# Expert tiles inside the late attention batches of a fused attention and mixture-of-experts kernel

## The chip, the core and the metric

One NeuronCore of a Trainium2 chip runs the whole program. The metric is the device time in microseconds (us) of one execution. PE is TensorE, DVE is VectorE, ACT is ScalarE, POOL is GpSimd, SP is SyncE.

## What is computed

The input x has 8 batches of 256 positions with 256 features in fp32. The output is x plus an attention branch plus a mixture-of-experts branch, both fed with the layer-normalised x:

```
xn  = layernorm(x)
qkv = xn @ Wqkv.T + b              # 16 query heads of 16; one key head and one value head of 16
A   = softmax(causal(q k^T / 4)) v @ out_w.T + out_b
p   = softmax(xn @ w_router.T);  top 4 of 16 experts, weights normalised to sum 1
M   = sum over chosen e of coeff_e * (silu(xn @ w_gate[e]) * (xn @ w_up[e])) @ w_down[e]
out = x + A + M
```

There are 2048 tokens and four choices for each. The choices are sorted by expert into tiles of 128 rows, of which there are MT = 79 at most.

## The kernel before

The program is written by hand, engine by engine, with counted semaphores. An engine runs its list strictly in order. It has three stages.

Front (0 to about 88 us). `normalise`, `project` and the router work in four groups of 512 tokens. Keys go to DRAM as `k_d`, queries as `q_d`, normalised rows as `xn_d`. SP loads keys back in two transfers of four pieces (`load_k`, L330), and POOL copies them out, five and four times, into `ks` (`copy_k`, L472). `load_q` (L335) loads a batch's queries in eight issues of 128 KB. DVE's routing (`choose`, `sum_over_tiles`, `slot_numbers`) ends the front.

Attention (about 88 to 217 us). `batch(b)` runs over 8 batches of NB = 12 slots. In each slot s, PE does one score block for the row maxima of a batch that is 18 slots ahead (`scores_for_max`, L638; DVE takes its maximum, L1194) and one score block of this batch (`scores`, L653; ACT takes Exp, L925). The first kind alternates between PSUM banks 0 and 1, the second between banks 3 and 4. Between them stand, at fixed slots: `weigh_v` (L664, s = 1, 5, 9), `context` (L676, s = 3, 8), `transpose_context` (L686, s = 1, 9), `project_out` (L692, s = 3, 11), `transpose_max` (L644, s = 7), and on ACT and DVE the copies that these need (`keep_context` L931, `keep_cxt` L936, `normalise_context`, `add_out`, `split_max`). `load_m` (L373) returns the maxima, and `load_q(b + 3)` follows when the scores of batch b are done. In slots 14 to 29 `list_rows` (L700) makes the lists of rows; POOL's one-hot tables for it (L499) have HOTS = 14 places in the room of the weights of experts 6 to 11. ACT issues the weights of two experts in each batch (`load_experts`, L951), three transfers of 512 KB.

Tile loop (221 to 486 us). For tile j: POOL gathers 128 rows (`gather`, L512); PE transposes them (`tile_xT`, L775), ACT copies them (L990); PE multiplies by gate and up weights of the tile's expert (`tile_gate_up`, L785); ACT takes Silu (`tile_silu`, L986); DVE multiplies by up and coefficient (`tile_h`, L1285); PE transposes (`tile_hT`, L793), DVE copies (L1292); PE multiplies by the down weights (`tile_down`, L801), two tiles behind; ACT copies (`tile_y`, L997); POOL adds the rows into `out` (even j) or `odd_d` (odd j) with an accumulating indirect transfer (`send`, L526). `gather(j)` waits until `tile_h` of tile j - 4 is done, and POOL's order is gather(j + 3), send(j - 2). `send(0)` waits until SP has stored x plus attention of all batches (L399). After the last send one accumulating transfer adds `odd_d` to `out` (L545).

Of the kernel before, what the change touches and what calls it, by code (L numbers as in the profile page):

```python
# [33 lines left out]
def attention_and_experts(nc, x, wqkv, bqkv, wout, bout, wrouter, wgate, wup, wdown, out):  # L34
# [22 lines left out]
    HOTS = 14  # L57
# [9 lines left out]
    q_d = nc.dram_tensor("q_d", (2 * B, 2, KC, P, HALF), F32).ap()  # L67
# [3 lines left out]
    with ExitStack() as ctx:  # L71
# [9 lines left out]
        with nc.sbuf_tensor("wgu_low", [P, (E - 4) * KC, 2 * F], F32) as wgu_low:  # L81
            with nc.sbuf_tensor("qs_wgu", [P, 2, H, HALF], F32R) as qs_wgu:
                pass
        wgu = sb("wgu", [P, E * KC, 2 * F])
        wdn = sb("wdn", [P, E * FC, D])
        HOT_E = 6
        hot = wgu[:, HOT_E * KC:(HOT_E + 6) * KC, :].rearrange("p r f -> p (r f)").bitcast(F16)
        hot_p = hot[:, 0:HOTS * TOP_K * P].rearrange("p (r k c) -> p r k c", r=HOTS, k=TOP_K)
        hot_j = hot[:, HOTS * TOP_K * P:HOTS * TOP_K * (P + MTE)].rearrange("p (r k c) -> p r k c", r=HOTS, k=TOP_K)
# [22 lines left out]
        after_q = sb("after_q", [P, NU, P])  # L112
        wqT = sb("wqT", [P, KC, D])
        wvrkT = sb("wvrkT", [P, KC, 48])
# [5 lines left out]
        stats = sb("stats", [P, NT, 6])  # L120
        mv = sb("mv", [P, NT, 2])
        var_e = sb("var_e", [P, NT])
        std0 = sb("std0", [P, NT])
        rstd = sb("rstd", [P, NT])
        logits = sb("logits", [P, NT, E])
        probs = sb("probs", [P, NT, E])
        rowstat = sb("rowstat", [P, NT])
        top_w = sb("top_w", [P, NT, 8])
        top_e = sb("top_e", [P, NT, 8], U32)
        top_ef = sb("top_ef", [P, NT, TOP_K])  # L130
        iota_e = sb("iota_e", [P, E])
        onehot = out_buf[:].rearrange("p (t k e) -> p t k e", t=NT, k=TOP_K)
        chosen = sb("chosen", [P, NT, E], BF16)
        PADT = NT // 2
        scan_t = sb("scan_t", [P, 2, PADT + NT, E])
        PADE = E // 2
        scan_e = sb("scan_e", [P, 2, PADE + E])
        ntile_i = sb("ntile_i", [P, E], I32)
        first_row = sb("first_row", [P, E])
        slot_i = sb("slot_i", [P, NT, TOP_K], I32)  # L140
        slot_p = sb("slot_p", [P, NT, TOP_K], I32)
        slot_f = sb("slot_f", [P, NT, TOP_K])
# [4 lines left out]
        tile_no = sb("tile_no", [1, MT])  # L147
        tile_ge = scan_t[0:1].rearrange("p a t e -> p (a t e)").bitcast(BF16)[:, 0:MT * E].rearrange("p (j e) -> p j e", j=MT)
        tile_ef = sb("tile_ef", [1, MT])
        tile_e = sb("tile_e", [1, MT], I32)  # L150
        slots = sb("slots", [P, MT], I32)
        get_row = sb("get_row", [P, MT], I32)

# [145 lines left out]
        def _(sp):  # L299
# [51 lines left out]
            for g in range(NG):  # L351
# [15 lines left out]
                if g == 1:  # L367
                    load_k(0, GW)
# [968 lines left out]
```

## Time and profile before

| | |
|---|---|
| time, median of 3 runs | 504.11 us (503.55 to 506.36) |
| the profiled execution's own time | 504.1 us |
| its span in the trace | 502.4 us |
| PE busy | 418.8 us, 83% |
| POOL busy | 294.8 us, 59% |
| DVE busy | 226.0 us, 45% |
| ACT busy | 179.8 us, 36% |
| transfers | 57.17 MB, mean 114 GB/s |

Busy times are sums over stages with different limits, so they don't say what bounds a stage. The chain of work that ended last does: it is followed back from the last instruction, at each step to what released it. Its shares are PE 36%, issue 19%, POOL 16%, DVE 12%, DMA 8%. "Issue" is time in which an engine waited for nothing that the profile shows.

### The profile page before, as it was taken

What the parts mean: (1) busy time and instruction counts of PE and PEld (TensorE: products, weight loads), DVE (VectorE), ACT (ScalarE), POOL (GpSimd) and SP (SyncE); (2) the same over time, 40 slices, a digit from 0 to 9 for tenths busy, and PEclk for the clock granted to TensorE, in tenths of its full rate; (3) what the DMA queues carried; (4) which work ended last, traced back from release to release, by engine and by line L of the source; (5) the groups of instructions that cost most, each with busy time, mean ns of one, the idle gap of its engine ahead of it and who ended that gap; (6) DMA issues with size and microseconds to landing.
All of it is one profiled execution on the core that took longest, in us unless ns stands there. A gap on an engine that the chain in (4) does not pass through costs nothing.

```text
span 502.4 us, 6742 instructions
## 1 busy us (share of the span) xinstructions
PE 418.8 (83%) x1672; PEld 227.8 (45%) x1673; DVE 226.0 (45%) x555; ACT 179.8 (36%) x424; POOL 294.8 (59%) x298
## 2 busy tenths in 40 slices
PE   4896083888889888879899999999999999999920
PEld 2242031434544544435565555555555555555510
DVE  5987688468767666413232222222222222222210
ACT  2353100337745556633333333333333333333310
POOL 7953130998511100303888888888888888888740
PEclk9889555559999999999999999999999999999985
DMA  7668796344876792642544444454544455446217
GB/s 218 228 180 189 179 131 97 126 80 136 167 151 165 179 187 86 213 147 64 78 76 81 82 79 77 77 82 76 84 74 75 84 85 82 75 77 81 38 22 146
DMA packets 54034, 57.17 MB, mean 114 GB/s; under 512 B 11376, under 2 KB 48928, under 8 KB 53760
## 3 DMA queue, kind: packets, MB, share of 16 engines
q0 software_dynamic: 15440, 21.51, 25.6%
q1 hardware_dynamic: 25904, 22.87, 20.9%
q10 hardware_dynamic: 12672, 12.58, 8.4%
q8 instruction: 7, 0.11, 0.1%
q14 instruction: 11, 0.09, 0.1%
HBM read 37.40 MB, written 23.33 MB: 121 GB/s over the span
## 4 chain that ended last, share of the span: by engine, by line
PE 36%; issue 19%; POOL 16%; DVE 12%; DMA 8%; SPq 4%; ACT 3%; ACTq 0%; POOLq 0%
POOL late L512 10%; PE bank L785 9%; PE bank L801 5%; PE bank L664 4%; PE bank L638 4%; PE bank L653 4%; POOL odd_d L526 3%; PE bank L692 3%; DVE pmax L1194 3%; POOL out_dram L526 3%; DMA late<-xn_d,get_row 2%; PE bank L676 2%; DVE early L1051 2%; PE bank L775 2%; DMA q_d<-early 2%
## 5 line engine op out<-in xcount | busy, mean ns | idle before, releaser
L785 PE MATMUL bank<-wgu,late 128*128 x316 | 152.2, 604 | 3.0 <-issue 1.2
L512 POOL DMA_INDIRECT late<-xn_d,get_row x79 | 83.2, 1053 | 69.2 <-PE bank L653 27.6
L1285 DVE SCALAR_TENSOR_TENSOR late<-late,bank 128x256 f32<-128x256 f32 x79 | 37.9, 480 | 154.5 <-ACT late L986 154.5
L925 ACT ACTIVATE pt<-bank 128x512 f32<-128x512 f32 x96 | 56.0, 599 | 79.3 <-PE bank L653 78.3
L801 PE MATMUL bank<-wdn,late 128*128 x316 | 81.5, 381 | 1.4 <-DVE late L1292 1.4
L1194 DVE TRANSPOSE_TENSOR_REDUCE pmax<-bank 128x16 f32<-128x512 f32 x96 | 66.5, 706 | 33.7 <-PE bank L638 32.7
L986 ACT ACTIVATE late<-bank 128x256 f32<-128x256 f32 x79 | 30.3, 383 | 130.8 <-PE bank L785 130.8
L785 PEld LDWEIGHTS bank<-wgu,late 128*128 128x128 f32 x316 | 53.7, 189 | 46.7 <-issue 45.5
L526 POOL DMA_INDIRECT out_dram<-late,slots x40 | 63.5, 1588 | 19.1 <-issue 10.4
L526 POOL DMA_INDIRECT odd_d<-late,slots x39 | 61.9, 1587 | 12.8 <-issue 9.8
L801 PEld LDWEIGHTS bank<-wdn,late 128*128 128x128 f32 x316 | 53.9, 190 | 6.4 <-issue 2.4
L499 POOL TENSOR_SCALAR wgu<-iota_p,slot_pf 128x128 f16<-128x128 f32 x64 | 38.8, 622 | 18.5 <-DVE slot_jf L1177 18.3
L1292 DVE COPY late<-bank 128x256 f32<-128x256 f32 x79 | 33.5, 424 | 33.4 <-PE bank L793 33.3
L997 ACT ACTIVATE late<-bank 128x256 f32<-128x256 f32 x79 | 30.3, 383 | 39.4 <-PE bank L801 39.4
L775 PEld LDWEIGHTS bank<-ident,late 128*128 128x128 f32 x158 | 19.2, 140 | 54.4 <-DMA late<-xn_d,get_row 43.9
L638 PE MATMUL bank<-qs_late,ks 96*128 96x512 f32 x60 | 33.5, 573 | 12.2 <-DVE pmax L1194 11.5
L472 POOL CAST ks<-wdn 64x640 fp32r<-64x640 f32 (+1 forms) x16 | 10.4, 675 | 47.5 <-PE bank L653 40.9
L775 PE MATMUL bank<-ident,late 128*128 128x128 f32 x158 | 31.9, 284 | 4.4 <-DMA late<-xn_d,get_row 4.3
L638 PE MATMUL bank<-qs_wgu,ks 96*128 96x512 f32 x36 | 20.8, 584 | 15.5 <-DVE early L1118 10.8
L990 ACT ACTIVATE late<-bank 128x256 f32<-128x256 f32 x79 | 30.0, 380 | 5.3 <-PE bank L775 4.8
L793 PE MATMUL bank<-ident,late 128*128 128x128 f32 x158 | 30.2, 273 | 0.0
L664 PE MATMUL bank<-pt,v_all 128*32 128x512 f32 x192 | 28.2, 661 | 0.0
(149 smaller groups left out, 413.8 us busy)
## 6 DMA issues: line engine op xcount, KB each, us to landing
qs_late<-q_d SPq DMA_DIRECT2D x40, 128.0 KB, 4.9
q_d<-early SPq DMA_DIRECT2D x16, 256.0 KB, 3.8
wgu<-in_L_ffn_w_gate_dram ACTq DMA_DIRECT2D x8, 512.0 KB, 4.2
wgu<-in_L_ffn_w_up_dram ACTq DMA_DIRECT2D x8, 512.0 KB, 4.4
wdn<-in_L_ffn_w_down_dram ACTq DMA_DIRECT2D x8, 512.0 KB, 3.3
qs_wgu<-q_d SPq DMA_DIRECT2D x24, 128.0 KB, 4.7
xs<-in_L_attn_x_dram SPq DMA_DIRECT2D x4, 512.0 KB, 3.9
odd_d<-scan_t SPq DMA_DIRECT2D x1, 2048.0 KB, 10.6
```

The source lines that it names most:

```text
L499: pool.tensor_scalar(hot_p[:, t % HOTS, c], iota_p[:], slot_pf[:, t, c:c + 1], None, ALU.is_equal).then_inc(hot_p_ready, 1)
L512: pool.indirect_dma_start(xg[:, j % RING, :], None, xn_d, bass.IndirectOffsetOnAxis(ap=get_row[:, j:j + 1], axis=0), bounds_check=last_row ...
L526: pool.indirect_dma_start(odd_d if j % 2 else out_rows, bass.IndirectOffsetOnAxis(ap=slots[:, j:j + 1], axis=0), ys[:, j % RING, :], None, ...
L638: pe.matmul(bank[:, N % 2, :], k, q, start=True, stop=True).then_inc(p1_ps, 1)
L664: mm = pe.matmul(bank[32 * j:32 * j + 32, 5, :], v_all[:, 2 * b + kt, :], weights[:, j], start=(kt == 0), stop=(g != 1), skip_group_check= ...
L775: t = pe.transpose(bank[:, 7, c * P:(c + 1) * P], xg[:, r, c * P:(c + 1) * P], ident[:, :])
L785: mm = pe.matmul(bank[:, 2 + buf, :], xT[:, buf, c, :], wgu[:, bass.ds(e * KC + c, 1), :], start=(c == 0), stop=(c == KC - 1))
L801: mm = pe.matmul(bank[:, 4 + buf, 0:D], hT[:, buf, c, :], wdn[:, bass.ds(e * FC + c, 1), :], start=(c == 0), stop=(c == FC - 1))
L925: act.activation(pt[:, G % 2, n % NU, :], bank[:, 3 + N % 2, :], ACT.Exp).then_inc(exp_done, 1)
L1194: dve.tensor_reduce(found, bank[:, N % 2, :].rearrange("p (h q) -> p h q", h=H), AX.X, ALU.max, apply_transpose=True).then_inc(max_done, 1)
L1285: dve.scalar_tensor_tensor(out=hh[:, buf, :], in0=hh[:, buf, :], scalar=xg[:, r, bass.ds(e + D, 1)], in1=bank[:, 2 + buf, F:2 * F], op0=AL ...
L1292: dve.tensor_copy(hT[:, buf].rearrange("p c t -> p (c t)"), bank[:, 6, 0:F]).then_inc(hT_ready, 1)
```

## The change

A third of a tile is put into each slot of batches 4 to 7 (EB = 4), so that EA = 16 tiles are worked there and the loop starts at tile 16. On each engine `tile_part(b, s)` does part s % 3 of tile j: part 0 is gate and up (PE), Silu (ACT) and the copy of the transposed h of tile j - 1 (DVE); part 1 is down of tile j - 1 and the transpose of the rows of tile j + 1 (PE), the two copies (ACT) and h (DVE); part 2 is the transpose of h (PE). For that room in PSUM the score blocks for maxima use bank 0 alone from block 66 on (`p1_bank`), and the scores of batches 4 to 7 bank 3 alone (`p2_bank`): each block waits until the one before it has been read.

Around it: `load_k` reads keys from DRAM straight into `ks`, repeated by the transfer (eight issues for a batch), `copy_k` goes; `load_q` takes four issues for a batch instead of eight, from a `q_d` of another order. ACT issues 27 smaller weight transfers (13 experts) before tile 0, four ahead of batch 0 and one in every second slot of batches 0 to 3, and five in batch 7. The one-hot tables have HOTS = 8 places in memory of their own, and `list_rows` is spread over slots 12 to 34. DVE finds the experts of tiles in batch 1. SP no longer stores x plus attention at the end: batches 0 to 2 are stored in batch 3, the rest of `out` is zeroed in the front, and POOL adds batches 3 to 7 with accumulating transfers just ahead of sends 5, 9, 13, 17 and 21, waiting for each.

The diff, cut to its core:

```diff
-    HOTS = 14
+    HOTS = 8
+    LATE_E = 13
+    EB = B // 2
+    EA = (B - EB) * NB // 3
+    STORED = 3
...
+        def list_step(t):
+            return NB + (3 * t) // 2
...
+        LIST = {list_step(t): t for t in range(NT)}
...
+        P1_LAST = EB * NB + NB + NB // 2
+
+        def p1_bank(N):
+            return N % 2 if N < P1_LAST else 0
+
+        def p1_free(N):
+            return N - 1 if N < P1_LAST else N
+
+        P2_LAST = EB * NB
+
+        def p2_bank(N):
+            return 3 + (N % 2 if N < P2_LAST else 0)
+
+        def p2_free(N):
+            return N - 1 if N < P2_LAST else N
...
+        ADD_BASE = {5: 3, 9: 4, 13: 5, 17: 6, 21: 7}
...
+            def load_k(b, kt):
+                first, n = (NU + 1, NU) if kt else (0, NU + 1)
+                keys = k_d[:, :, b * S + kt * P:b * S + (kt + 1) * P]
+                for a in range(2):
+                    for r in range(2):
+                        at = 32 * a + 16 * r
+                        sp.dma_start(ks[at:at + 16, b % KBUF, first:first + n].bitcast(F32),
+                                     keys[a].unsqueeze(1).to_broadcast([HD, n, P])).then_inc(k_in[b % KBUF][kt], 16)
 
             def load_q(b, half):
-                for r in range(4):
-                    sp.dma_start(qs[b % 3][16 * r:16 * r + 16, half].rearrange("p (m h) t -> p m (h t)", m=KC).bitcast(F32),
-                                 q_d[2 * b + half, r % 2].rearrange("m (d h) t -> d m (h t)", d=HD)
+                for r in range(2):
+                    sp.dma_start(qs[b % 3][32 * r:32 * r + 32, half].rearrange("p h t -> p (h t)").bitcast(F32),
+                                 q_d[2 * b + half].rearrange("a (d h) m t -> (a d) (h m t)", d=HD)
                                  ).then_inc(q_in[b % 3][half], 16)
 
+            def load_batch(b):
+                for half in range(2):
+                    load_k(b, half)
+                    load_q(b, half)
 
             def store_xn(g):
                 sp.wait_ge(xn_ready, GT * (g + 1))
...
+                         zeros.unsqueeze(1).to_broadcast([P, NT - STORED * S // P, D])).then_inc(zeroed, 16)
 
             store_xn(0)
...
+                    load_batch(0)
...
+            sp.wait_ge(k_stored, 32 * NG)
+            load_batch(1)
...
                 if b + 3 < B:
                     sp.wait_ge(s_ps, (b + 1) * NB)
...
-                sp.wait_ge(o_added, 2 * (stop // S))
...
-                             xs[:, start // P:stop // P, :]).then_inc(base_stored, 16)
-            sp.wait_ge(base_stored, 32)
+                    load_batch(b + 3)
+                if b == 1:
+                    sp.wait_ge(part_e_ready, 2)
+                    sp.dma_start(tile_e[:, :], part_e[0:MT, :]).then_inc(tile_e_in, 16)
+                if b == STORED:
+                    sp.wait_ge(o_added, 2 * STORED)
+                    sp.dma_start(out_rows[0:STORED * S].rearrange("(u p) d -> p u d", p=P), xs[:, 0:STORED * S // P, :]
...
-                elif j == 1:
-                    pool.wait_ge(odd_zeroed, 16)
-                else:
+                    pool.wait_ge(base_stored, 16)
+                    pool.wait_ge(zeroed, 32)
+                if j >= 2:
                     pool.wait_ge(y_sent[(j - 2) % RING], 16 * ((j - 2) // RING + 1))
+                if j in ADD_BASE:
+                    b = ADD_BASE[j]
+                    pool.wait_ge(o_added, 2 * (b + 1))
+                    pool.dma_start((odd_d if j % 2 else out_rows)[b * S:(b + 1) * S, :].rearrange("(u p) d -> p u d", p=P),
+                                   xs[:, 2 * b:2 * b + 2, :], accum_op=ALU.add).then_inc(base_added, 16)
+                    pool.wait_ge(base_added, 16 * (b - STORED + 1))
...
                     pe.wait_ge(qs_padded, 2 * (b % 3) + n // NU + 1)
+                if n == 2 * NU:
+                    pe.wait_ge(k_in[b % KBUF][1], 64 * (b // KBUF + 1))
...
+                    pe.wait_ge(max_done, p1_free(N))
                 k, q = queries(b, n, 96)
-                pe.matmul(bank[:, N % 2, :], k, q, start=True, stop=True).then_inc(p1_ps, 1)
+                pe.matmul(bank[:, p1_bank(N), :], k, q, start=True, stop=True).then_inc(p1_ps, 1)
 
             def transpose_max(b):
                 pe.wait_ge(max_joined, b + 1)
...
+            def keep_row(j):
+
+                pe.wait_ge(gathered[j % RING], 16 * (j // RING + 1))
+                if j > 1:
...
+            def tile_part(b, s):
+                j, part = tile_at(b, s), s % 3
+                if part == 0:
+                    if j == 0:
+                        pe.wait_ge(experts_in, 16 * N_EARLY)
+                        pe.wait_ge(max_done, P1_LAST)
+                    pe.wait_ge(xgT_ready, j + 1)
+                    if j:
+                        pe.wait_ge(h_ready, j)
...
+                                       start=(c == 0), stop=(c == KC - 1))
+                    mm.then_inc(gu_ps, 1)
+                if part == 1:
+                    if j:
...
+                        pe.wait_ge(exp_done, P2_LAST)
+                        if j > 1:
+                            pe.wait_ge(y_ready, j - 1)
+                        for c in range(FC):
+                            mm = pe.matmul(bank[:, 4, 0:D], hT[:, (j - 1) % 2, c, :],
+                                           wdn[:, bass.ds(ds[j - 1] * FC + c, 1), :],
+                                           start=(c == 0), stop=(c == FC - 1))
+                        mm.then_inc(dn_ps, 1)
+                    keep_row(j + 1)
+                if part == 2:
+                    pe.wait_ge(h_ready, j + 1)
+                    pe.wait_ge(xgT_ready, j + 2)
+                    for c in range(FC):
...
+                    t.then_inc(hT_ps, 1)
+                    if j + 1 < EA:
+                        es[j + 1] = expert(j + 1)
+                    ds[j] = expert_down(j)
...
                     scores(b, s)
-                    if 0 <= b * NB + s - LIST_AT < NT:
-                        list_rows(b * NB + s - LIST_AT)
...
+                    if b >= EB:
+                        tile_part(b, s)
...
+            def load_early(n):
+
+                pair, which = divmod(n, 4)
+                e0, e1 = 2 * pair, min(2 * pair + 2, LATE_E)
+                if which < 2:
+                    act.dma_start(wgu[:, e0 * KC:e1 * KC, which * F:(which + 1) * F],
+                                  (wgate, wup)[which][e0:e1].rearrange("e (c p) f -> p (e c) f", p=P)
+                                  ).then_inc(experts_in, 16)
+                else:
+                    e = e0 + which - 2
+                    act.dma_start(wdn[:, (E - 1 - e) * FC:(E - e) * FC, :], wdown[e].rearrange("(c p) f -> p c f", p=P)
+                                  ).then_inc(experts_in, 16)
...
+            def tile_part(b, s):
+                j, part = tile_at(b, s), s % 3
+                if part == 0:
+                    act.wait_ge(gu_ps, j + 1)
+                    act.activation(hh[:, j % 2, :], bank[:, 1, 0:F], ACT.Silu).then_inc(silu_ready, 1)
+                if part == 1:
+                    if j:
+                        act.wait_ge(dn_ps, j)
+                        if j > RING:
+                            act.wait_ge(y_sent[(j - 1) % RING], 16 * ((j - 1) // RING))
+                        act.activation(ys[:, (j - 1) % RING, :], bank[:, 4, 0:D], ACT.Copy).then_inc(y_ready, 1)
+                    keep_row(j + 1)
...
-                        load_experts(B - 2 + s // 5, 2)
-                    if b == B - 1 and s < 4:
...
+                        tile_part(b, s)
+                    if (b, s) == (EB - 1, NB - 1):
+                        keep_row(0)
+                    if b < EB and (b * NB + s) % 2 == 1 and 4 + (b * NB + s) // 2 < N_EARLY:
...
+                        load_late(s)
                     if b:
                         if s == 1:
                             keep_cxt(b - 1, 0)
...
+            def tile_part(b, s):
+                j, part = tile_at(b, s), s % 3
+                if part == 0 and j:
+                    dve.wait_ge(hT_ps, j)
+                    dve.tensor_copy(hT[:, (j - 1) % 2].rearrange("p c t -> p (c t)"), bank[:, 2, D:D + F]).then_inc(hT_ready, 1)
+                if part == 1:
+                    e = dve.value_load(tile_e[0:1, 2 * j:2 * j + 1], min_val=0, max_val=E - 1)
+                    dve.wait_ge(silu_ready, j + 1)
+                    dve.scalar_tensor_tensor(out=hh[:, j % 2, :], in0=hh[:, j % 2, :],
+                                             scalar=xg[:, j % RING, bass.ds(e + D, 1)],
+                                             in1=bank[:, 1, F:2 * F], op0=ALU.mult, op1=ALU.mult
+                                             ).then_inc(h_ready, 1)
 
...
```

## Rows read from the trace of the kernel before

**Rows 1.** Page: clock in 40 slices; groups: busy us, mean ns, idle before them.
```profile
PEclk9889555559999999999999999999999999999985
L925 ACT ACTIVATE pt<-bank 128x512 f32<-128x512 f32 x96 | 56.0, 599 | 79.3 <-PE bank L653 78.3
L1194 DVE TRANSPOSE_TENSOR_REDUCE pmax<-bank 128x16 f32<-128x512 f32 x96 | 66.5, 706 | 33.7 <-PE bank L638 32.7
L986 ACT ACTIVATE late<-bank 128x256 f32<-128x256 f32 x79 | 30.3, 383 | 130.8 <-PE bank L785 130.8
```
**Rows 2.** Stretches: start:end length, busy PE PEld DVE ACT POOL, clock, DMA share, GB/s.
```profile
153.00:168.00 15.00, 13.23 (x70) 7.29 (x69) 10.32 (x23) 8.20 (x16) 1.27 (x2) 1.00 0.76 166
395.00:435.00 40.00, 39.01 (x147) 22.31 (x146) 10.85 (x24) 13.11 (x37) 32.35 (x26) 1.00 0.49 79
```
**Rows 3.** Timeline of GpSimd in the tile loop: start, length, instruction, idle before it.
```profile
234.40 1.64 POOL L526 DMA_INDIRECT out_dram<-late,slots  x1 [5.97 <-ACT late L997]
236.34 1.05 POOL L512 DMA_INDIRECT late<-xn_d,get_row  x1 [0.30 <-issue]
...
471.61 1.59 POOL L526 DMA_INDIRECT odd_d<-late,slots  x1 [0.31 <-issue]
```
**Rows 4.** Chain that ended last, one tile of the loop: start, length, what.
```profile
371.32 1.72 PE bank L785 x4
...
373.43 0.87 PE bank L801 x4
374.30 0.22 PE bank L793 x2
...
376.23 0.22 PE bank L775 x2
```
**Rows 5.** The same chain within attention, batches 3 and 4.
```profile
154.95 0.24 PE bank L638
155.19 0.24 PE bank L653
...
160.86 0.99 PE bank L664 x8
...
163.88 0.66 PE bank L676 x4
164.53 0.87 PE bank L692 x4
```
**Rows 6.** The same chain: ends of batches 3 and 7, first tile.
```profile
158.78 1.13 PE bank L692 x4
...
215.46 1.15 PE bank L692 x4
...
221.31 1.99 PE bank L785 x4
```
**Rows 7.** Timeline of ScalarE where it changes from Sqrt to Exp.
```profile
37.69 1.28 ACT L864 ACT_TABLE_LOAD   x1
38.99 0.26 ACT L864 ACTIVATE probs<-logits 128x64 f32<-128x64 f32 x1
```
**Rows 8.** Timeline of SyncE's queue: issues of transfers, start, length of all of them.
```profile
38.46 3.25 SPq L330 DMA_DIRECT2D wdn<-k_d  x4
...
43.15 4.28 SPq L335 DMA_DIRECT2D qs_wgu<-q_d  x8
...
106.50 3.57 SPq L335 DMA_DIRECT2D qs_wgu<-q_d  x8
```
**Rows 9.** Chain that ended last: the wait for batch 1's queries.
```profile
65.64 7.12 DMA qs_late<-q_d
```
**Rows 10.** Transfers by line: queue, count, KB each, median us to landing.
```profile
out_dram<-odd_d POOLq DMA_DIRECT2D x1, 2048.0 KB, 12.7
late<-xn_d,get_row POOLq DMA_INDIRECT x79, 2.9
out_dram<-late,slots POOLq DMA_INDIRECT x40, 3.8
```

More of the change, by code:

```diff
@@ L168, in carve @@
                 at += n
-            assert at <= WORK
             return found
@@ L380, in _ @@
             sp.wait_ge(vrT_ps, NG)
-            for half in range(2):
-                load_q(1, half)
+            sp.wait_ge(k_stored, 32 * NG)
+            load_batch(1)
             sp.wait_ge(q_stored, 64 * NG)
@@ L387, in _ @@
             sp.dma_start(xn_d[:, D:D + E].rearrange("(t p) e -> p t e", p=P), logits[:]).then_inc(coef_stored, 16)
-            for half in range(2):
-                load_q(2, half)
+            load_batch(2)
             for b in range(B - 1):
@@ L702, in list_rows, with tile_xT, expert, expert_down @@
                 mm.then_inc(list_ps, 1)
+            def tile_xT(j, r, came):
+                pe.wait_ge(gathered[r], came)
+                for c in range(KC):
+                    t = pe.transpose(bank[:, 0, c * P:(c + 1) * P], xg[:, r, c * P:(c + 1) * P], ident[:, :])
+                t.then_inc(xgT_ps, 1)
+            def expert(j):
+                return pe.value_load(tile_e[0:1, bass.ds(2 * j, 1)], min_val=0, max_val=E - 1)
+            def expert_down(j):
+                return pe.value_load(tile_e[0:1, bass.ds(2 * j + 1, 1)], min_val=0, max_val=E - 1)
@@ L818, in tiles @@
                         last_output(u)
+                    if first and u == 1:
+                        pe.wait_ge(ct_ready, 2 * B)
                     if not (first and u == 0):
@@ L924, in exp_scores @@
                     act.wait_ge(pv_ps, G - 1)
-                act.activation(pt[:, G % 2, n % NU, :], bank[:, 3 + N % 2, :], ACT.Exp).then_inc(exp_done, 1)
+                act.activation(pt[:, G % 2, n % NU, :], bank[:, p2_bank(N), :], ACT.Exp).then_inc(exp_done, 1)
             def keep_context(b, qt):
@@ new lines, in tile_silu, with tile_xT, tile_y @@
+            def tile_silu(j, buf):
+                act.wait_ge(gu_ps, j + 1)
+                act.activation(hh[:, buf, :], bank[:, 1 + buf, 0:F], ACT.Silu).then_inc(silu_ready, 1)
+            def tile_xT(j, buf):
+                act.wait_ge(xgT_ps, j + 1)
+                act.activation(xT[:, buf].rearrange("p c t -> p (c t)"), bank[:, 0, 0:D], ACT.Copy
+                               ).then_inc(xgT_ready, 1)
+            def tile_y(j, r, sent):
+                act.wait_ge(dn_ps, j + 1)
+                if sent is not None:
+                    act.wait_ge(y_sent[r], sent)
+                act.activation(ys[:, r, :], bank[:, 3 + r % 2, 0:D], ACT.Copy).then_inc(y_ready, 1)
@@ L977, in batch @@
                         keep_context(b, 0)
+            for n in range(4):
+                load_early(n)
             for b in range(B):
```

383 lines of the change are left out of this document (176 added, 207 removed).

## The prediction

> **What bounds the kernel now.** I read the clock and the groups first, then the stretches, the timeline of GpSimd, and the chain.
>
> The stretches show two stages that both keep PE busy: 13.2 of 15 us in attention and 39.0 of 40 us in the tile loop [rows 2]. Busy is not bound. In the loop POOL never rests: a gather takes 1.05 us, a send 1.59, with 0.3 of issue before each. From the first send to send 73 there are 73 tiles in 237.2 us, 3.25 us each [rows 3]. PE alone needs 1.72 for gate and up, 0.87 for down and 0.22 for each of two pairs of transposes, 3.03 us a tile [rows 4]. So the loop is bound by POOL, by 0.22 us a tile.
>
> In attention at full clock PE's order decides. A batch holds 24 score blocks at 0.24 us, three `weigh_v` at 1.00, two `project_out` at 0.87, two `context` at 0.44 (0.66 where it comes after a wait), two `transpose_context` at 0.22 and a 0.1 us transpose [rows 5, 4]: 11.9 us. Batches 4 to 7 run from 159.9, the end of batch 3's last projection, to 216.6, the end of the last one before the tail of attention [rows 6]: 56.7 us. The last 18 slots have no block for maxima (4.3 us less), so PE's own work is 4 x 11.9 - 4.3 = 43.3 us and 13.4 us are waits on copies and maxima. Those waits are what the change can fill.
>
> **The tiles inside attention.** Sixteen tiles bring 16 x 3.03 = 48.5 us of PE work. With no wait at all the four batches would take 91.8 us. They will not, since each score block now waits for the reader of the one before, and ACT must go from Exp to Silu and back for every tile. Where ACT goes from Sqrt to Exp it loads a table for 1.28 us, and the next activation starts 0.02 us later [rows 7]. No row shows Exp and Silu under one table, so I take two loads a tile.
>
> I walk one tile through its three slots, from the start of the first block for maxima (M), with Exp 0.60, row maximum 0.71 and Silu and other copies 0.38 [rows 1]. A block is read 0.40 us after its start. Part 0: M 0 to 0.24, scores (S) to 0.48, gate and up to 2.20. ACT: Exp 0.68 to 1.28, load to 2.56, Silu to 2.94, load to 4.22. Part 1 on PE: M, S, down, transposes, from 2.20 to 3.77; ACT: Exp 4.22 to 4.82, the two copies to 5.50. Part 2: S waits for that Exp, 4.86 to 5.10; the transpose of h waits for the second copy, 5.54 to 5.76; ACT's Exp 5.50 to 6.10. The next S waits for it and starts at 6.14, where this one's started at 0.24: 5.9 us. ACT, not PE (4.5 us), closes the cycle.
>
> The other work of attention stands in this frame. That of part 0 (s = 3, 9) and part 1 (s = 1) runs on PE while ACT loads or copies, at 0 to 0.3 us; that of part 2 shows (s = 5, 8, 11: 1.0, 0.44, 0.87), but takes the last wait's place; ACT's `keep_context` and `keep_cxt` add up to 0.6. Walked so, the four tiles of a batch take 6.1, 7.0, 6.7 and 6.8 us, 26.6 together. Four batches: 106.4, less 1.2 where blocks for maxima lack (only those that nothing hides), plus 0.15 a tile because a weight load after a wait shows (`context` 0.66 for 0.44 [rows 5]): 107.6 us. Bounds: 91.8 (all waits covered), and 118, if the 13.4 us of old waits stay beside the new ones.
>
> On ScalarE's loads the Trainium skill speaks against the row. "ScalarE: Activation LUTs", section "What ACT_TABLE_LOAD costs", gives about 1283 ns for the load and 1380 ns of drain, 2.66 us for each switch, and advises to batch by table set. The first figure agrees with the row; the drain does not show in it [rows 7].
>
> **From attention to tile 16.** Before, 4.7 us lie between the last projection and the first gate [rows 6]. After, a transpose, a copy, a projection, `weigh_v`, a copy and `context` stand there: about 0.4 + 0.6 + 0.87 + 1.0 + 0.8 + 0.44 = 4.1. Tile 16 starts its gate at 159.9 + 107.6 + 4.1 = 271.6, plus what the front adds.
>
> **The loop.** It has 63 tiles. POOL is caught up on entry, since tiles came every 6.7 us. Send 16 waits for the copy of y(16), behind two gates, the late down of tile 15 and its own down: about 9.5 us after tile 16's gate starts. From there POOL sets 3.25 us a tile as before: send 73 comes 57 x 3.25 = 185.3 us later. PE at 3.03 stays hidden. To this come two base additions (before sends 17 and 21; those before 5, 9 and 13 are hidden, since a tile there lasts twice POOL's 3.25). POOL issues a 256 KB accumulating transfer and waits until it has landed. The nearest rows: a gather lands in 2.9 us, a send of 128 KB in 3.8, the 2048 KB one in 12.7 [rows 10]. Between the last two, (12.7 - 3.8) / 15 = 0.6 for 128 KB more makes 4.4; without the send's longer issue I take 4.2 each, bounds 2.9 and 5.4: 8.4 us. After send 73 the rest is as before: 502.4 - 471.6 = 30.8 [rows 3].
>
> **The front and batches 0 to 3.** (a) SP's chain at 38 to 50 us loses four key issues (3.25 us) and four query issues (half of 4.28) and gains eight key issues at about 0.45 [rows 8]: -1.8, of which the transfer traffic (keys are now repeated in flight) takes back some: -1.5. (b) Batch 1's queries landed in 7.1 us and were waited for [rows 9]. SP now issues eight keys and four queries there, while ACT puts 1.5 MB of weights on the same engines: between -1 and +4, taken as +1. (c) Keys and queries of batches 3 to 5 are issued when a ring buffer is freed, six slots (about 7.5 us) before use. The first half of the queries stands behind four key issues (1.9 us), and weights go up from 1.5 to 2.5 MB a batch at a DMA share of 0.76 already [rows 2]: 0 to +4, taken as +1. (d) Tile 0 waits for the 27th weight transfer, issued two slots before: 0 to +4, +1.5. (e) Zeroing 1.25 MB, the moved list, its eight places, the routing table of experts in batch 1 and ACT's issues hide behind PE in batches that POOL and DVE don't bound [rows 2]; POOL's copies of keys weren't waited for. If that cover fails, some tenths of a us for each. Half clock in batch 0 [rows 1] stays as it is. Sum +2.0, bounds -2 and +11.
>
> **Sum.** 271.6 + 9.5 + 185.3 + 8.4 + 30.8 + 2.0 = 507.6 us of span. Around the span the profiled execution has 1.7 us (504.1 against 502.4), so 509.3, say 509. That execution stands at the median of the three runs, 504.11.
>
> **Rivals.**
> 1. The score blocks don't stall and the walk is too strict. The waits of 13.4 us go and few new ones come, as in the loop, where PE is busy 39 of 40 us [rows 2]: about 96 us in place of 107.6, 497. For it: DVE and ACT have spare time in these batches. Against: both bank pairs are now single. It decides once the four batches, the front's change included, take less than 104 us. Chance 0.20, and faster.
> 2. One table serves both functions. Then the same walk gives 25.0 us a batch (6.05, 6.9, 5.2, 6.8), since PE's work fills what ACT leaves: 6.4 us less, 503. No row speaks for it or against. Chance 0.20.
> 3. Transfers come late: the bounds of (b), (c) and (d) at once, +7 more, 516. For it the share of 0.76 [rows 2]. Against: fewer and longer pieces for queries. Chance 0.15.
> 4. Each change of function costs ACT twice what the row shows, because the engine must empty first and the row falls where it was empty already. Two more times 1.28 for a tile are 41 us, of which PE's own work hides little: about 546. The row's 0.02 us after the load speaks against it. Chance 0.03. By the drain that the Trainium skill gives, named above, it would be 16 x 2 x 1.38 = 44 us instead of 41.
> The forecast, 504 to 513, has 0.42.
>
> **Range and chances.** More than 0.5% from 504.1, 2.5 us, is about what a measurement of this kernel tells from no change. Faster: rival 1 and a part of 2, 0.28. Same: most of 2 and the forecast's low end, 0.21. Slower: the rest, 0.51. The range, 496 to 519, takes in rivals 1, 2 and 3; the forecast's own is 504 to 513.
>
> **What would show it.** The table loads counted on ACT (32 more, or one); batches 4 to 7 at 26 to 27 us each; send 16 some 8 us earlier than the old one at 234.4 + 16 x 3.25 = 286.4; POOL at 3.25 again, with two gaps of about 4 us; the first scores of batch 4 within 3 us of 160. The prediction is wrong if PE rests less than 10 us in batches 4 to 7, if the clock falls there, or if tile 0 waits long for weights.

## The result and the profile after

| | before | after |
|---|---|---|
| time, median | 504.53 us (503.55 to 506.36) | 541.42 us (539.55 to 543.93) |
| ratio after / before, 95% interval | | 1.073 (1.067 to 1.079) |
| the profiled execution: time, span | 504.1, 502.4 us | 543.93, 542.2 us |
| end of batch 3's last projection | 159.9 us | 165.0 us |
| batches 4 to 7 | 56.7 us | 132.5 us |
| send 16 | 286.4 us | 313.2 us |
| send 16 to send 73 | 185.2 us | 194.8 us |
| send 73 to the end | 30.8 us | 34.2 us |

The change costs 7%; the forecast, 509.0 with 496 to 519, was wrong in size and right in sign. Against the forecast's own sum (span 507.6) the profiled execution is 34.6 us longer: front +3.1, batches 4 to 7 +24.9 (132.5 for 107.6), from there to the gate of tile 16 +1.0, from that gate to send 16 +1.1, the loop +1.1, after send 73 +3.4. (The profiled execution is the slowest of the kernel's four, 2.5 us above their median.)

The page of the kernel after, the lines that answer to [rows 1] (the first line here is PE's busy share in the same 40 slices):

```profile
PE   4793363888797888887878889799999999999910
PEclk9898555789878989899997998899999999999975
L998 ACT ACTIVATE pt<-bank 128x512 f32<-128x512 f32 x96 | 57.0, 599 | 95.2 <-PE bank L672 93.7
L1300 DVE TRANSPOSE_TENSOR_REDUCE pmax<-bank 128x16 f32<-128x512 f32 x96 | 67.5, 711 | 70.8 <-PE bank L657 69.8
L780 PE MATMUL bank<-wgu,short 128*128 x64 | 35.3, 680 | 0.2 <-ACT short L1053 0.2
L739 PE MATMUL bank<-wgu,short 128*128 x252 | 122.5, 609 | 1.7 <-issue 1.3
```

No operation has become dearer on ACT or DVE. But gate and up inside attention (L780) take 680 ns a matmul and the same work in the loop (L739) 609, and of the ten slices from 163 to 298 us three have the clock at 8 tenths and one at 7, where before all had 9 [rows 1].

ACT's groups in 160 to 300 us, then its timeline around one tile (start, length, instruction):

```profile
L1060 ACT ACT_TABLE_LOAD x16 | 20.5, 1283 | 0.3
L998 ACT ACT_TABLE_LOAD x16 | 20.5, 1283 | 0.3
```
```profile
184.57 1.28 ACT L1060 ACT_TABLE_LOAD   x1
185.86 0.38 ACT L1060 ACTIVATE short<-bank 128x256 f32<-128x256 f32 x1
186.15 0.59 ACT L1004 ACTIVATE ct<-bank 128x512 f32<-128x512 f32 x1
186.75 1.28 ACT L998 ACT_TABLE_LOAD   x1
188.05 0.60 ACT L998 ACTIVATE pt<-bank 128x512 f32<-128x512 f32 x1
```

Two loads a tile, 32 in all, each 1.28 us as in [rows 7]. Each starts 0.02 us behind the activation before it, and the next activation starts 0.01 to 0.02 us behind the load wherever its input is there. So rivals 2 and 4 fall, and the loads are priced as forecast.

The chain of the kernel after, from the start of batch 4 (start, length, what):

```profile
167.96 0.39 ACT short L1060
168.34 0.02 issue
168.36 1.28 ACT L998
169.65 0.01 issue
169.66 0.61 ACT pt L998
170.26 0.04 issue
170.31 0.50 PE bank L672
170.81 0.27 PE bank L799 x2
171.08 2.04 issue
173.12 0.67 PE bank L657
173.79 0.43 PE bank L672
174.22 3.01 PE bank L780 x4
...
189.34 0.41 PE bank L799 x2
189.75 1.00 issue
190.75 1.08 PE bank L695 x4
```

Up to 170.81 this is the forecast's walk. Then comes what it had not: behind the transpose of h (L799) PE is idle for 1.0 us, once 2.0, and waits for nothing that the profile shows. The code has two reads of registers there, which give the experts of the next tile's gate and of this tile's down. PE's waits between 165 and 297 us name ten such pauses, 10.2 us in all. (Four more waits of 1.0 us there, before `weigh_v`, L683, are put down to ACT's Exp. They go too once the reads are moved, in e1.) Then gate and up take 3.01 us where [rows 4] has 1.72; the granted clock between 174 and 176 us is 0.50.

### The profile page after: what moved, and what is told of

Read it like the earlier page. It is cut to its first block, busy times and chain, and to the rows that moved or that the text cites. A ratio compares the mean times of both kernels' runs of the same rounds, so it can differ in the third digit from the quotient of the medians.

```text
span 542.2 us, 6885 instructions
## 1 busy us (share of the span) xinstructions
PE 428.1 (79%) x1672; PEld 234.8 (43%) x1673; DVE 223.0 (41%) x557; ACT 221.4 (41%) x456; POOL 291.7 (54%) x287
## 4 chain that ended last, share of the span: by engine, by line
PE 36%; issue 18%; POOL 11%; DMA 11%; DVE 10%; ACT 7%; SPq 3%; ACTq 0%; POOLq 0%; DVEq 0%
PE bank L739 7%; POOL short L524 5%; PE bank L780 4%; PE bank L755 4%; PE bank L683 4%; PE bank L657 3%; PE bank L672 3%; DMA short<-xn_d,get_row 3%; POOL out_dram L543 3%; ACT pt L998 2%; POOL odd_d L543 2%; PE bank L710 2%; DMA qs_late<-q_d 2%; DVE pmax L1300 2%; DVE early L1156 2%
## 5 line engine op out<-in xcount | busy, mean ns | idle before, releaser
L524 POOL DMA_INDIRECT short<-xn_d,get_row x79 | 84.3, 1067 | 127.3 <-DVE short L1354 82.2
L739 PE MATMUL bank<-wgu,short 128*128 x252 | 122.5, 609 | 1.7 <-issue 1.3
L1337 DVE SCALAR_TENSOR_TENSOR short<-short,bank 128x256 f32<-128x256 f32 x63 | 30.3, 480 | 122.9 <-ACT short L1038 113.4
L543 POOL DMA_INDIRECT odd_d<-short,slots x39 | 62.2, 1595 | 28.2 <-DMA odd_d<-xs 16.2
L543 POOL DMA_INDIRECT out_dram<-short,slots x40 | 63.5, 1586 | 17.2 <-issue 8.6
L755 PE MATMUL bank<-wdn,short 128*128 x256 | 67.0, 385 | 1.4 <-DVE short L1344 1.4
L1038 ACT ACTIVATE short<-bank 128x256 f32<-128x256 f32 x63 | 24.2, 384 | 105.6 <-PE bank L739 104.0
L739 PEld LDWEIGHTS bank<-wgu,short 128*128 128x128 f32 x252 | 43.8, 194 | 35.8 <-issue 35.5
L515 POOL TENSOR_SCALAR short<-iota_p,slot_pf 128x128 f16<-128x128 f32 x64 | 38.3, 617 | 18.1 <-DVE slot_jf L1282 18.1
L755 PEld LDWEIGHTS bank<-wdn,short 128*128 128x128 f32 x256 | 44.1, 192 | 5.8 <-issue 2.4
L1049 ACT ACTIVATE short<-bank 128x256 f32<-128x256 f32 x64 | 24.6, 384 | 33.2 <-PE bank L755 27.6
L780 PE MATMUL bank<-wgu,short 128*128 x64 | 35.3, 680 | 0.2 <-ACT short L1053 0.2
L657 PE MATMUL bank<-qs_w,ks 96*128 96x512 f32 x36 | 22.0, 618 | 15.9 <-DVE early L1223 10.2
L683 PE MATMUL bank<-pt,v_all 128*32 128x512 f32 x192 | 28.4, 666 | 4.1 <-ACT pt L998 4.1
L657 PEld LDWEIGHTS bank<-qs_late,ks 96*128 96x128 f32 x60 | 13.6, 231 | 32.9 <-issue 24.2
## 6 DMA issues: line engine op xcount, KB each, us to landing
odd_d<-short SPq DMA_DIRECT2D x1, 2048.0 KB, 10.8
```

Source lines behind the costliest of these rows:

```text
L515: pool.tensor_scalar(hot_p[:, t % HOTS, c], iota_p[:], slot_pf[:, t, c:c + 1], None, ALU.is_equal).then_inc(hot_p_ready, 1)
L524: pool.indirect_dma_start(xg[:, j % RING, :], None, xn_d, bass.IndirectOffsetOnAxis(ap=get_row[:, j:j + 1], axis=0), bounds_check=last_row ...
L543: pool.indirect_dma_start(odd_d if j % 2 else out_rows, bass.IndirectOffsetOnAxis(ap=slots[:, j:j + 1], axis=0), ys[:, j % RING, :], None, ...
L657: pe.matmul(bank[:, p1_bank(N), :], k, q, start=True, stop=True).then_inc(p1_ps, 1)
L683: mm = pe.matmul(bank[32 * j:32 * j + 32, 5, :], v_all[:, 2 * b + kt, :], weights[:, j], start=(kt == 0), stop=(g != 1), skip_group_check= ...
L739: mm = pe.matmul(bank[:, 1 + buf, :], xT[:, buf, c, :], wgu[:, bass.ds(e * KC + c, 1), :], start=(c == 0), stop=(c == KC - 1))
```

## Experiments

The times of e1 to e6 are single executions, beside the kernel before at 503.01 (e1 to e4) and 502.13 us (e5, e6); e7 has ten, e8 and e9 have four. The stages are those of one traced execution each. All times and stages together, in us; "busy, idle" is PE's busy time in the stretch of batches 4 to 7, cut to whole us, and the rest of that stretch:

| | time | end of batch 3 | batches 4 to 7 | busy, idle | send 16 to 73 | last send to end |
|---|---|---|---|---|---|---|
| before | 504.1 | 159.9 | 56.7 | 48.6, 7 | 185.2 | 19.4 |
| after | 543.9 | 165.0 | 132.5 | 107.7, 24 | 194.8 | 22.8 |
| e1 | 520.5 | 162.4 | 111.0 | 100.9, 10 | 195.5 | 22.9 |
| e2 | 524.7 | 161.6 | 116.1 | 98.1, 17 | 195.4 | 22.8 |
| e3 | 512.9 | 163.1 | 103.0 | 97.5, 6 | 195.1 | 22.9 |
| e4 | 531.1 | 164.0 | 132.2 | | 186.3 | 19.8 |
| e5 | 538.0 | 163.4 | 60.9 | 51.1, 10 | 196.2 | 22.8 |
| e6 | 508.6 | 166.0 | 103.6 | | 188.6 | 20.1 |
| e7 | 503.9 | 162.4 | 103.1 | | 188.4 | 20.0 |
| e8 | 499.0 | 157.8 | 102.9 | 96.9, 5 | 188.5 | 20.1 |
| e9 | 526.9 | 158.4 | 67.8 | 54.1, 14 | 188.8 | 20.0 |

**e1: the register reads moved.**

```diff
                     mm.then_inc(gu_ps, 1)
+                    if j + 1 < EA:
+                        es[j + 1] = expert(j + 1)
+                    ds[j] = expert_down(j)
                 if part == 1:
...
                     t.then_inc(hT_ps, 1)
-                    if j + 1 < EA:
-                        es[j + 1] = expert(j + 1)
-                    ds[j] = expert_down(j)
```

> Edit: in the tiles inside attention PE reads the two expert numbers right behind the gate and up matmuls of part 0, where 1.7 us of work is queued, and no longer behind the transpose of h in part 2. Theory A (the 1.0 us of issue behind each of the 16 transposes of h is PE's sequencer reading registers with nothing queued): these gaps go, batches 4 to 7 take 132.4 - 16 x 0.8 = about 119 us, and the time falls by 11 to 15 us. Rival (the gap only covers ACT's Exp of part 2, which ends late because of the table loads): a wait for ACT of the same length takes its place, and the time falls by under 4 us.

Measured: 520.45 us, batches 4 to 7 in 111.0, 21.5 less; theory A had about 119, since it counted the pauses and not the clock. One move of two reads gives back most of the 24.9 us by which these batches miss the forecast. (Chance is no rival here: e4, whose code is that of the change up to send 16, repeats the 132 us.) The stretches of both kernels, from which the table's busy times are (start:end length, PE, PEld, DVE, ACT, POOL busy, clock, DMA share, GB/s), first after, then e1:

```profile
165.00:297.00 132.00, 107.73 (x447) 60.29 (x446) 44.20 (x97) 91.17 (x144) 44.83 (x34) 0.94 0.40 81
```
```profile
162.00:273.00 111.00, 100.86 (x449) 57.44 (x447) 44.21 (x98) 91.17 (x144) 44.16 (x34) 0.98 0.47 96
```

The same instructions, within two: PE is idle 14.1 us less (24.3 against 10.1), which is 16 tiles by 0.9, and busy 6.9 us less, because the clock rose from 0.94 to 0.98. So a pause costs itself and then a part of the matmuls behind it. The trace bears the size out: the clock stands at its lower level for 17.1 us of the kernel after's batches 4 to 7 and for 3.4 us of e1's, and half of the difference is 6.8. In finer stretches of the kernel after the clock drops where PE has rested, for a part of the stretch to its lower level (1.2 GHz, 0.5 in the row); in e1 it stays full from 185 to 195. First after, then e1:

```profile
185.00:195.00 10.00, 7.71 (x27) 4.79 (x25) 3.49 (x8) 6.63 (x10) 2.66 (x2) 0.83 0.19 31
285.00:289.00 4.00, 2.86 (x9) 1.88 (x10) 0.42 (x1) 1.49 (x4) 1.30 (x1) 0.62 0.59 97
289.00:293.00 4.00, 4.00 (x14) 1.34 (x12) 0.54 (x2) 2.45 (x4) 1.67 (x1) 0.53 0.27 28
```
```profile
185.00:195.00 10.00, 9.86 (x47) 5.84 (x49) 5.22 (x11) 8.42 (x13) 2.64 (x2) 1.00 0.33 66
```

**e2 and e3: no change of table**, alone and with e1's edit. Both leave out the Silu of the sixteen inner tiles, so their output is another.

```diff
-                    act.activation(hh[:, j % 2, :], bank[:, 1, 0:F], ACT.Silu).then_inc(silu_ready, 1)
+                    act.activation(hh[:, j % 2, :], bank[:, 1, 0:F], ACT.Copy).then_inc(silu_ready, 1)
```

> Edit: Silu of the 16 tiles inside attention is a Copy, so that ACT never leaves the Exp table there. What is left out: the Silu of these tiles. Theory B (the 32 table loads carry the loss): batches 4 to 7 fall from 132 us to under 112. Rival, by the walk of the prediction: PE's own work fills what ACT leaves, 1.6 us a batch, so 126 us at most 6 us less; with the register reads still there even less.

> Both edits together (the Silu of the 16 inner tiles is left out). If the two causes are separate, the gains add; if each hides the other, this run gains more than the sum of the two. By the walk without loads, batches 4 to 7 take 100 us and the time falls by about 30 us. If the granted clock in these batches falls because PE waits, it stays at 1.00 here.

Measured: e2's 116.1 us lie between theory B's 112 and the rival's 126, and e3's 103.0 are near the walk's 100. With the reads moved (e1 to e3) the 32 loads are worth 8.0 us in batches 4 to 7; the two walks of the prediction differ by 6.4. With the reads where the change has them (after to e2) the loads are worth 16.4, because there PE is also below full clock: e2's stretch has clock 1.00 and 9.6 us less busy time than the kernel after (98.1 for 107.7). Both repairs together give 29.5, less than 21.5 + 16.4: they share the clock's part, which either of them alone takes away nearly whole. With the clock at 1.00 throughout, e3's stretch of 103.0 us stands 5.5 us above the time that PE is busy in it:

```profile
163.00:266.00 103.00, 97.45 (x448) 56.84 (x446) 44.19 (x97) 50.65 (x112) 42.76 (x33) 1.00 0.49 102
```

**e4: the additions of batches 6 and 7 left out**, which the output then lacks.

```diff
-        ADD_BASE = {5: 3, 9: 4, 13: 5, 17: 6, 21: 7}
+        ADD_BASE = {5: 3, 9: 4, 13: 5}
```

> Edit: the additions of x plus attention of batches 6 and 7 ahead of sends 17 and 21 are left out, so the output lacks them. Theory: each stops GpSimd for 4.3 us in the loop that GpSimd bounds, so the time falls by 8 to 9 us. Rival: PE bounds the start of the loop and covers them, under 3 us.

Measured: sends 16 to 73 in 186.3 us instead of 194.8, 4.25 for each addition. GpSimd's timeline in the kernel after shows one of them; between a gather and its send there are 4.3 us more than the usual 0.3:

```profile
315.09 1.07 POOL L524 DMA_INDIRECT short<-xn_d,get_row  x1 [0.30 <-issue]
316.24 1.30 POOL L540 DMA_DIRECT2D odd_d<-xs  x1
320.75 1.66 POOL L543 DMA_INDIRECT odd_d<-short,slots  x1 [3.21 <-DMA odd_d<-xs]
322.71 1.09 POOL L524 DMA_INDIRECT short<-xn_d,get_row  x1 [0.30 <-issue]
```

After the last send the kernel also takes 3.0 us less than after, though the merging transfer lands in 12.7 us as before; see "Two small terms" below.

**e5: no tile inside.** `EB = B`, all else as in the change; all 79 tiles in the loop, score banks in pairs.

> Edit: every part of the change is kept (key, query and weight transfers, lists, zeroed output, five added sums), but no tile is worked inside attention: EB = B, the loop starts at tile 0 as before. It prices the rest of the change. Attention of batches 4 to 7 takes 57 us again at full clock. The end of batch 3 stays at 162 to 165 us, if transfers and not tiles delay it (159.9 before). All five additions now stand in the loop: 5 x 4.35 = 21.8 us, less 4 us for the first send that no longer waits for a store. Sum: 504.1 + 4 + 21.8 - 4 + 3 (the longer tail) = about 529 us. If it comes out near 504, the additions are hidden and the tiles inside carry all of the loss; near 541, the tiles inside cost nothing.

Measured: 537.95 us, far above the forecast. Batches 4 to 7 take 60.9 us for 56.7, the front 3.5 more, and five additions now stand in the loop: sends 0 to 73 take 262.1 us (239.78 to 501.89) for 237.2, 5.0 for each; the end takes 3.4 more. So moving the tiles inside costs the changed kernel at most 6.0 us of its 37 (543.93 against 537.95), 3.5 by the median of its four, and 1.1 if each is taken against the kernel before beside it (36.9 against 35.8). One execution of e5 can't tell these apart, as the four of the change spread over 4.4 us. That doesn't make the other 31 us the price of what lies around the tiles: without tiles inside, three additions more stand in the open.

**e6: mended.** e1's edit, each addition issued one send earlier and waited for where it was, the weights spread over slots 2 to 43, and Silu worked as 0.5 z (1 + tanh(z/2)), with Tanh on ACT and one more operation on DVE.

```diff
-                    act.activation(hh[:, j % 2, :], bank[:, 1, 0:F], ACT.Silu).then_inc(silu_ready, 1)
+                    act.activation(hh[:, j % 2, :], bank[:, 1, 0:F], ACT.Tanh, scale=0.5).then_inc(silu_ready, 1)
...
+                    dve.scalar_tensor_tensor(out=hh[:, j % 2, :], in0=hh[:, j % 2, :], scalar=1.0,
+                                             in1=bank[:, 1, 0:F], op0=ALU.add, op1=ALU.mult).then_inc(half_ready, 1)
+                    dve.wait_ge(half_ready, j + 1)
...
-                if j in ADD_BASE:
-                    b = ADD_BASE[j]
+                if j + 1 in ADD_BASE:
+                    b = ADD_BASE[j + 1]
                     pool.wait_ge(o_added, 2 * (b + 1))
+                    pool.wait_ge(y_sent[(j - 1) % RING], 16 * ((j - 1) // RING + 1))
...
-                    pool.wait_ge(base_added, 16 * (b - STORED + 1))
+                if j in ADD_BASE:
+                    pool.wait_ge(base_added, 16 * (ADD_BASE[j] - STORED + 1))
```

> Four edits to the changed kernel, each in a stage of its own, so that the trace prices each: register reads of PE behind gate and up (as in e1_regs); silu(x) of the inner tiles as x/2 (1 + tanh(x/2)), Tanh on ACT, one more operation on DVE, and the factor 1/2 in the copy of y; the added sums issued one send earlier, so that a send and a gather cover their landing; no weight transfer ahead of batch 0, and all 27 spread over slots 2 to 43. Theory B: if Exp and Tanh share a table, no table load is seen inside and batches 4 to 7 take 103 us as in e3; if they don't, 111 as in e1. Additions: from 4.35 us each in the loop to about 1.9, send 16 to send 73 from 195 to 190. Transfers: batch 1's queries land 2 to 3 us earlier (75.1 in the changed kernel, 72.8 before), batch 3 ends near 160. Time 504 to 508 us. Rival: the later weights wait at tile 0, and what the front gains is lost there.

Measured: 508.62 us, just above the expected 504 to 508, with batches 4 to 7 in 103.6. ACT loads three tables in the whole kernel, as many as before the change: Exp and Tanh stand in one. The Trainium skill says so too ("ScalarE: Activation LUTs", section "Table sets: the hidden batching unit"), and the trace agrees. The front didn't gain.

Sends 16 to 73 take 188.6 us for 194.8, but they hold only one whole addition now, since the one before send 17 is issued ahead of send 16. The whole one, for send 21, widens the gap between two sends from 3.25 to 6.0 us and the next gap to 3.5, so an early addition costs 3.0 us, not 4.3, in a loop that GpSimd bounds: it waits 1.4 us until the send before has landed, then issues for 1.3. In e8:

```profile
292.47 1.29 POOL L544 DMA_DIRECT2D odd_d<-xs  x1 [1.42 <-DMA odd_d<-short,slots]
294.07 1.66 POOL L548 DMA_INDIRECT out_dram<-short,slots  x1 [0.31 <-issue]
```

**e7: the weights back where the change has them.** Else as e6.

> The kernel of e6 with the weights of the experts issued as the changed kernel issues them (four ahead of batch 0, one in every second slot of batches 0 to 3). Register reads behind gate and up, Silu by Tanh, base additions one send early stay. Theory T (weights and keys share the transfer engines, and whichever is issued first the queries wait): spreading them otherwise gave nothing in e6, so the end of batch 3 stays at 165 to 166 and the time at 507.5 to 509.5. Rival U (e6's spreading did hurt or help by itself): end of batch 3 below 163.5 or above 168, time outside 506 to 511.

Measured: 503.88 us (502.19 to 506.89), before 503.79; ratio 1.0012 (0.9988 to 1.0036). The expectation of theory T fell: batch 3 ends at 162.4 us, and the time is 4.7 us below e6's. What e6's spreading costs is less sure than that. e6 ran once, 1.7 us above the slowest of e7's ten, and its 166.0 is close to what kernels with e7's placing of the weights show: after, e1 to e5 and e7 end batch 3 between 161.6 and 165.0. With three repairs and everything else of the change in place, the 7% are gone.

**e8: few weights first.**

```diff
-            for n in range(4):
-                load_early(n)
...
-                    if b < EB and (b * NB + s) % 2 == 1 and 4 + (b * NB + s) // 2 < N_EARLY:
-                        load_early(4 + (b * NB + s) // 2)
+                    if 1 <= b < 3 and s % 3 == 1:
+                        load_early((b - 1) * 4 + s // 3)
+                    if b >= EB and s % 3 < 2 and FIRST + 2 * ((b - EB) * NB // 3 + s // 3) + s % 3 < N_EARLY:
+                        load_early(FIRST + 2 * ((b - EB) * NB // 3 + s // 3) + s % 3)
```

The first FIRST = 8 transfers count on a semaphore of their own, and tile 0 waits for that one. They are the weights of experts 0 to 3, all that the sixteen inner tiles need with this input; for another input the kernel leaves out a wait that it would need.

> As e7, but only the 8 weight transfers of experts 0 to 3, which are all that the sixteen tiles inside need with this input, are issued before tile 0 (in batches 1 and 2); the other 19 follow in batches 4 to 6 and tile 0 doesn't wait for them. Theory T (the front's 5 us are transfers in each other's way): the DMA share of 108 to 143 us falls from 0.9 to 0.7, batch 3 ends at 161 to 163 in place of 165 to 166, the time is 504 to 507. Rival V (it is the keys' own repeated transfer and SP's issues, not the weights): batch 3 ends at 164.5 or later, time as e7 within 1 us. Rival W (the gain comes back in batches 4 to 7, where the 19 transfers now meet gathers and sends): batches 4 to 7 take over 105.5 us for 103.6.

Measured: 498.98 us (498.19 to 499.65), ratio to before 0.991 (0.988 to 0.994): 0.9% faster than the kernel before. Batch 3 ends at 157.8 us, even 2.1 before the old kernel's; e9, with the same front, has 158.4, and the seven kernels with the change's placing of weights have 161.6 or more. Rival W falls: the 19 transfers in batches 4 to 7 cost nothing there (102.9 us). SyncE's queue shows where the early weights stand in the way. First the kernel after, then e8, the issues for batch 1 (start, length of all):

```profile
61.18 2.44 SPq L362 DMA_DIRECT2D ks<-k_d  x4
63.66 1.12 SPq L367 DMA_DIRECT2D qs_late<-q_d  x2
64.82 5.06 SPq L362 DMA_DIRECT2D ks<-k_d  x4
69.92 0.89 SPq L367 DMA_DIRECT2D qs_late<-q_d  x2
```
```profile
60.83 2.48 SPq L365 DMA_DIRECT2D ks<-k_d  x4
63.35 0.93 SPq L370 DMA_DIRECT2D qs_late<-q_d  x2
64.32 1.83 SPq L365 DMA_DIRECT2D ks<-k_d  x4
66.19 0.89 SPq L370 DMA_DIRECT2D qs_late<-q_d  x2
```

In the kernel after, ScalarE issues four weight transfers (1.5 MB) between 58.7 and 61.2 us; in e8 none before batch 1. With them, four issues of keys take SyncE 5.06 us instead of 1.83, the first queries of batch 1 land in 10.94 us (7.12 before [rows 9]), and PE waits 3.4 us for them, where e8 has no such wait. The stretch of 60 to 75 us, after and then e8:

```profile
60.00:75.00 15.00, 7.90 (x12) 3.10 (x12) 11.42 (x30) 0.00 (x0) 3.73 (x2) 0.50 0.94 243
```
```profile
60.00:75.00 15.00, 10.27 (x16) 4.11 (x16) 13.31 (x36) 0.00 (x0) 3.72 (x2) 0.50 0.65 146
```

PE gets through 12 blocks in the one and 16 in the other. The DMA share alone (0.94, 0.65) doesn't tell why: the kernel before has 0.96 there and gets through 17, with no weights in front of the queries.

But PE's wait of 3.4 us is not what the front loses in the end. The last projection of batch 2 ends at 143.8 us in the kernel after, 143.9 in the kernel before and 142.7 in e8. All 5.1 us come in batch 3: PE waits 2.2 us for returned maxima, and then the clock falls. The wait, then 146 to 156 us of the kernel after, of the kernel before and of e8:

```profile
146.22 0.79 PE L672 MATMUL bank<-qs_w,ks 98*128 98x512 f32 x1 [2.19 <-DMA qs_w<-nm]
146.00:156.00 10.00, 9.46 (x28) 5.59 (x29) 2.48 (x4) 3.15 (x6) 4.34 (x4) 0.50 0.97 186
146.00:156.00 10.00, 8.72 (x49) 4.93 (x41) 7.09 (x16) 6.12 (x12) 0.00 (x0) 1.00 0.85 201
146.00:156.00 10.00, 8.73 (x47) 4.93 (x47) 6.65 (x16) 5.18 (x11) 3.66 (x4) 1.00 0.75 162
```

**e9: few weights first, no tile inside.** e8 with `EB = B`; its 19 later weight transfers stay in batches 4 to 7.

> As e8, but no tile inside attention: all 79 tiles in the loop, the bank pairs of the score blocks stay pairs. Everything else of the change and of e8 stays (keys by transfer, weights in e8's places, five base additions one send early). It prices the sixteen tiles inside where nothing else is wrong. Theory (they are worth what the walk says: sixteen times 3.25 us of loop, 52.0, against about 102.5 - 57 = 45.5 us more in batches 4 to 7, and three base additions of 1.1 us which then show): 499.0 + 6.5 + 3.3 = 508.8, range 506.5 to 511. Rival (the gain of e8 over the kernel before comes from the front alone, and the tiles inside bring nothing): 499 to 501, with batches 4 to 7 at 57 us and send 0 at 232.

Measured: 526.88 us (525.83 to 527.62), 28 above e8 and far beyond both expectations. From batch 3's end to send 16 it takes 147.1 us, where the theory had 130.1 (57 + 17.8 + 52.0 + 3.3). Of the 17 more, batches 4 to 7 make 10.8 (67.8 us) and the first sixteen sends 8.5; 2.3 come back between. In batches 4 to 7 PE waits for returned maxima (4.7 us in two waits), and the clock is not full, as it isn't in the loop's beginning:

```profile
158.00:226.00 68.00, 54.08 (x260) 28.44 (x259) 30.35 (x67) 32.79 (x64) 0.00 (x0) 0.92 0.74 192
240.00:300.00 60.00, 53.38 (x195) 31.46 (x195) 14.42 (x32) 17.51 (x50) 44.43 (x34) 0.94 0.51 77
```

The rival falls: e8's gain doesn't come from the front alone. But e9 gives no clean price of the sixteen tiles. The 8.5 us of the sends are the additions, which the theory priced too low: four of them stand there (before sends 5, 9, 13 and 17), and the sixteen gaps take 63.9 us for 52.0, so 3.0 for each as in e6, where the theory had three at 1.1. And e9 changes the room of the 19 late transfers together with the tiles: in e8 they lie in 103 us that PE fills, here in 57 that wait on copies. e5, which has them in batches 0 to 3, needs 60.9 us there, 6.9 less. That makes the transfers the likely cause of most of the 10.8, but no run moves them alone, so it stays open; the sum below puts the tiles at 6.

## Why the prediction was wrong

- **The walk's part 2 failed.** This step cost the forecast most. It lets PE go from the transpose of h (5.76) to the next score block (6.14) with only ACT to wait for. The two register reads that stand there in the code, though not in its list of instructions, take 1.0 us each tile with PE's queue empty: 16 x 0.9 = 14 us that the sum had at nothing. The walk's upper bound of 118 (by its own terms 107.6 + 13.4 = 121) was passed too, at 132.5.
- **The clock was taken as full from batch 1 on.** The prediction named "if the clock falls there" as a way to be wrong, and gave it no price or chance. It fell, and the same instructions kept PE busy 6.9 us longer than in e1. The reads moved (e1) end that nearly, the loads gone (e2) wholly, so it is pauses and loads together that the walk should have carried into the clock.
- **Otherwise the walk held.** 107.6 forecast, 111.0 in e1; about 101 without loads (4 x 25.0 - 1.2 + 2.4), 103.0 in e3 and 102.9 in e8. It says rightly that ACT's loads, not PE, close a tile's cycle, and rival 1 (PE covers the waits) is wrong with loads in. The load's price of 1.28 held, and the doubled one of rival 4 did not.
- **The front.** +2.0 forecast, +5.1 measured, within its bounds of -2 and +11, but not by its terms. Term (b), batch 1's queries, was sized at +1, and the wait for them is 3.4 us against 0.5 before. By 143.8 us it is made good, in part by luck: between 90 and 105 us the kernel after has a mean clock of 0.73, the kernel before 0.50, though the prediction let batch 0's clock stay as it is. What is left comes in batch 3, from 2.2 us of waiting for returned maxima, which had no term, and from the clock at 0.50 for the 10 us behind it. So the clock failed the forecast here as well. Rival 3, transfers late, thus happened in part; e8 and e9 show that the weights issued ahead of batch 4 are the cause. (Rival 3's "+7 more" is 8.5 by its own bounds, 12 against the 3.5 in the sum.)
- **The additions.** 4.2 each forecast, 4.25 measured in e4: right, by the interpolation between the 128 KB send and the 2048 KB merge [rows 10], whose bounds of 2.9 and 5.4 were wide. What the prediction wanted to see, send 16 some 8 us earlier than 286.4, is 3.3 us by its own sum (271.6 + 2.0 + 9.5 = 283.1); it came at 313.2.
- **Two small terms.** From batch 7 to send 16 the sum has 13.6 us and the trace 15.7. After send 73 "as before" is 3.4 us off. The merging transfer takes as long as before, the end of the program comes 6.7 us behind its landing for 3.3. The kernels with five additions waited for at once have it (22.8), e4 with three and e6 to e9 with early ones don't (19.8 to 20.1). Why is open.
- **What was forecast in the wrong proportion.** The prediction took the sixteen tiles as the matter and the rest as small change. In e8 the sum against the kernel before is: front -2.1, batches 4 to 7 and the sixteen tiles 102.9 - (56.7 + 52.0) = -5.8, from there to the first send of the loop 17.3 for 17.8, the loop's addition +3.3, end +0.7: -4.4, as the spans differ. What sixteen tiles inside bring, where nothing spoils it, is thus 6 us; the register reads (21.5), the two late additions (8.5) and the table loads (8.0) each cost more.

## What to carry to other kernels

Before walking an engine's order, list everything in its program, register reads and the like too, and ask of each whether the engine's queue is empty when it comes: put them behind the longest run of matmuls, not behind the short one that everybody waits for. Price a new pause on TensorE twice, once as itself and once as the clock that it may take from the matmuls behind it. And issue only those weights early that the early work needs.

## What the runs showed of the hardware that was not expected

- Two register reads on PE behind a 0.4 us transpose leave it idle for 0.9 to 1.0 us (eight times in the kernel after, and once each for 2.0 and 0.3 us); behind 1.72 us of gate and up one such pause is left in the list of e1.
- In the kernel after, the granted clock was 0.83 from 185 to 195 us, with PE idle for 2.3 of the 10 us, and 0.62 from 285 to 289, with 1.1 of 4 us idle; from 289 to 293 it was 0.53, nearly all at the lower level, though PE never rested. The longest rest in batches 4 to 7 was 2.0 us. With the reads moved (e1) or the loads gone (e2) the mean of batches 4 to 7 is 0.98 and 1.00 instead of 0.94.
- Four issues of keys on SyncE took 5.06 us where ScalarE had just issued 1.5 MB of weights, and 1.83 without.
- An accumulating transfer of 256 KB, waited for at once, takes GpSimd 4.3 us: 1.30 to issue and 3.21 of waiting behind it, less the usual 0.3 between two instructions. Issued one send earlier it takes 3.0: 1.4 of waiting for the send before, 1.3 to issue, and 0.3 behind it.
- A table load on ScalarE starts 0.02 us behind the activation before it and doesn't wait for the input of the next: in the tile of 193.34 us it is over 0.4 us before the gate and up matmuls that its Silu needs.
